# Cross-attention and mixture-of-experts layer: the residual travels with the scattered token rows and is added on VectorE instead of by an accumulating scatter

## The reference

```python
x = x + _L0_xattn_ref(_layernorm(x), ctx_1024, Wq1, Wk1, Wv1, Wk2, Wv2, Wo, bo)
x = x + _L0_ffn_ref(_layernorm(x), shared_w1, shared_w2, expert_w1, expert_w2, router_w, ln_gamma, ln_beta)
# _L0_ffn_ref:
h = (x - mu) / jnp.sqrt(var + LN_EPS) * ln_gamma + ln_beta
shared_out = jax.nn.silu(h @ sw1.T) @ sw2.T            # sw, ew: weights rounded to -1, 0, 1 times a row scale
probs = jax.nn.softmax(h @ router_w.T, axis=-1)
gate = one_hot(argmax(probs)) * max(probs)
h1 = jax.nn.silu(jnp.einsum('btd,efd->ebtf', h, ew1))
eo = jnp.einsum('ebtf,edf->ebtd', h1, ew2)
return shared_out + jnp.einsum('ebtd,bte->btd', eo, gate)
```

## Time and profile before

| what | us |
|---|---|
| median of 3 runs (lowest to highest) | 825.51 (825.13 to 829.35) |
| the profiled execution's own time | 822.83 |
| its span | 821.0 |
| PE busy | 674.1 (82%) |
| DVE busy | 640.7 (78%) |
| ACT busy | 586.1 (71%) |
| POOL busy | 578.7 (70%) |

### The profile page before, as it was taken

One profiled execution on the slowest core, in us unless ns is written; L12 is line 12 of the kernel. 1 busy time (PEld: TensorE's weight loads), 2 busy tenths in 40 slices (PEclk: granted clock), 3 DMA queues, 4 the chain that ended last, 5 costly groups with the idle time before them and its releaser, 6 DMA issues.

```text
span 821.0 us, 22257 instructions
## 1 busy us (share of the span) xinstructions
PE 674.1 (82%) x7738; PEld 471.7 (57%) x7738; DVE 640.7 (78%) x1411; ACT 586.1 (71%) x1324; POOL 578.7 (70%) x684
## 2 busy tenths in 40 slices
PE   3689779899989998999889898989997555777883
PEld 2355546666666666666656565766664343655652
DVE  3878768889888988788888888888977647676873
ACT  3668667888787878788787878787876622665662
POOL 1356557787878778697888787878877755365664
PEclk9989999999999999999999999999998877899997
DMA  7289867898998998979998889999795913699991
GB/s 256 39 170 161 174 125 151 167 172 184 171 173 169 167 180 170 187 156 181 175 175 166 162 172 170 175 179 177 138 165 136 165 45 119 129 143 142 149 132 15
DMA packets 367523, 126.87 MB, mean 155 GB/s; under 512 B 331114, under 2 KB 362740, under 8 KB 367412
## 3 DMA queue, kind: packets, MB, share of 16 engines
q1 hardware_dynamic: 359604, 116.11, 74.2%
q0 software_dynamic: 7232, 8.79, 7.2%
q10 hardware_dynamic: 576, 0.54, 0.2%
HBM read 30.71 MB, written 14.71 MB: 55 GB/s over the span
## 4 chain that ended last, share of the span: by engine, by line
PE 31%; DVE 20%; issue 14%; DMA 11%; SPq 9%; ACT 8%; POOL 6%; DVEq 0%; ACTq 0%; POOLq 0%
PE FB L358 10%; DMA pt<-p_split 8%; PE TBK L1463 4%; DVE neg_max L1208 4%; PE S L1391 4%; SPq L514 4%; POOL p_split L582 3%; ACT p_split L784 2%; DVE FB L946 2%; SPq L507 2%; DVE above L951 2%; ACT k_st L747 2%; DVE v_st L976 2%; DVE hn L1058 2%; SPq L508 2%
## 5 line engine op out<-in xcount | busy, mean ns | idle before, releaser
L582 POOL TENSOR_TENSOR p_split<-probs,p_split 128x512 f16<-128x512 f32 x256 | 300.6, 1183 | 62.8 <-ACT p_split L784 60.2
L822 ACT ACTIVATE probs<-S,neg_max 128x512 f32<-128x512 f32 x256 | 175.3, 685 | 16.1 <-DVE neg_max L1208 14.8
L784 ACT ACTIVATE p_split<-probs 128x512 f16<-128x512 f32 x256 | 161.1, 629 | 16.0 <-DMA pt<-p_split 14.5
L1208 DVE TENSOR_REDUCE neg_max<-S 128x1 f32<-128x512 f32 x256 | 171.1, 679 | 0.3
L358 PE MATMUL FB<-xt_hi,w_split 128*128 128x256 f16 x768 | 141.6, 276 | 3.2 <-DVE xt_lo L973 2.9
L1407 PE MATMUL O<-v_st,pt 128*128 128x64 f16 x1024 | 114.8, 195 | 23.0 <-DMA pt<-p_split 22.9
L1407 PEld LDWEIGHTS O<-v_st,pt 128*128 128x128 f16 x1024 | 93.3, 99 | 56.4 <-DMA pt<-p_split 32.8
L1408 PE MATMUL O<-v_st,pt 128*128 128x64 f16 x1024 | 114.1, 194 | 0.0
L1409 PE MATMUL O<-v_st,pt 128*128 128x64 f16 x1024 | 114.1, 194 | 0.0
L1391 PE MATMUL S<-k_st,q_st 64*128 64x512 f16 x768 | 107.1, 385 | 1.1 <-ACT probs L822 1.1
L358 PE MATMUL FB<-xt_lo,w_split 128*128 128x256 f16 x384 | 105.8, 276 | 0.0
(11 more groups left out here) (223 smaller groups left out, 1752.4 us busy)
## 6 DMA issues: line engine op xcount, KB each, us to landing
w_raw<-in_L_ffn_expert_w SPq DMA_DIRECT2D x16, 512.0 KB, 4.4
w_split<-rows SPq DMA_DIRECT2D x39, 132.0 KB, 2.5
c_in<-in_ctx SPq DMA_DIRECT2D x16, 256.0 KB
x_in<-in_x SPq DMA_DIRECT2D x16, 256.0 KB
xb<-in_x SPq DMA_DIRECT2D x16, 256.0 KB, 3.3
pt<-p_split SPq DMA_TRANSPOSE x256, 3.3
out<-rest SPq DMA_DIRECT2D x15, 256.0 KB, 2.7
k_st<-in_L_xattn_Wk SPq DMA_DIRECT2D x2, 512.0 KB, 7.1
```

The source lines that it names most:

```text
L582: g.tensor_tensor(p_split[n % HL_RING][:, 1, :], probs[n % PROBS_RING][:, :], p_split[n % HL_RING][:, 0, :], ALU.subtract).then_inc(p_lo_r ...
L784: a_(p_split[g % HL_RING][:, 0, :], probs[g % PROBS_RING][:, :], ACT.Copy).then_inc(p_hi_ready, 1)
L822: a_(probs[n % PROBS_RING][:, :], S[n % 4][:, :], ACT.Exp, bias=neg_max[:, n % 4:n % 4 + 1], accum_out=sums[:, n % UNITS:n % UNITS + 1]).t ...
L1208: v.tensor_reduce(neg_max[:, n % 4:n % 4 + 1], S[n % 4][:, :], AX.X, ALU.max, negate=True)\
```

## The change

The rows in device memory become twice as wide: HALF = 264 floats as before, and behind them another 264 that begin with the token's residual part. `rest` is gone: DVE and POOL write the residual part into `row`, and it is scattered with the rest of the row. The stores of the residual part to `out` are gone (L496, L699), so nothing is in `out` before the expert stage; DVE adds the residual part to each tile's result (`add_residual`) and POOL scatters it without adding. `scatter_rows` now needs the residual part, so the table moves the scatters of the last batch but one (EARLY_SCATTER 44 to 46). The last batch is scattered in two halves: the first half at once, the residual half when it is ready. The ring of row buffers has the same memory and so half the places (RING 16 to 8). Tiles 0 to 7 are loaded by halves, the first by SP, the second by POOL behind the last scatter; the others by SP as one load of 264 KB. The zero rows are twice as wide too. In the expert stage ACT scales three of the four chunks and DVE one.

```diff
-RING = 16
+RING = 8
-EARLY_COUNT, EARLY_RANKS, EARLY_PLACE, EARLY_SCATTER = 40, 41, (42, 43), 44
+EARLY_COUNT, EARLY_RANKS, EARLY_PLACE, EARLY_SCATTER = 40, 41, (42, 43), 46
-    rows = nc.dram_tensor("rows", [E * ROOM, WIDTH], F32, kind="Internal").ap()
+    rows = nc.dram_tensor("rows", [E * ROOM, 2 * HALF], F32, kind="Internal").ap()
...
-                t = due(n, STORE_R)
-                if t is not None and t < B - 1:
-                    sp.wait_ge(r_ready, t + 1)
-                    sp.dma_start(out_v[t], rest[t % 2][:, :, :]).then_inc(r_stored, 16)
...
             def load_rows(a):
                 at = sp.value_load(tile_row[0:1, bass.ds(a, 1)], min_val=0, max_val=E * ROOM - P)
-                sp.dma_start(g_rows[a % RING], rows[bass.ds(at, P), :]).then_inc(row_in[a % RING], 16)
+                cols = HALF if a < RING else 2 * HALF
+                sp.dma_start(g_rows[a % RING][:, 0:cols], rows[bass.ds(at, P), 0:cols]).then_inc(row_in[a % RING], 16)
...
-                sp.dma_start(rows[bass.ds(at, P), :], zeros).then_inc(padded, 16)
+                sp.dma_start(rows[bass.ds(at, P), :].rearrange("p (k c) -> p k c", k=2), pad_rows).then_inc(padded, 16)
...
                     if a + LEAD >= RING:
+                        if a + LEAD == RING:
+                            sp.wait_ge(r_scattered, 16 * TB)
                         sp.wait_ge(e_out, a + LEAD - RING + 1)
...
+                    pool.wait_ge(r_ready, t + 1)
                 scatter(row[t % 2][:, i, :], rows, dest_at[:, t * TB + i:t * TB + i + 1], E * ROOM - 1)\
                     .then_inc(scattered[t % 2], 16)
...
             pool.wait_ge(r_ready, B)
-            g.dma_start(out=out_v[B - 1], in_=rest[(B - 1) % 2][:, :, :]).then_inc(last_r_stored, 16)
-            pool.wait_ge(r_stored, 16 * (B - 1))
-            pool.wait_ge(last_r_stored, 16)
+            pool.wait_ge(halves_ready, 2)
+            for i in range(TB):
+                scatter(row[(B - 1) % 2][:, i, HALF:2 * HALF], half_rows, half_at[:, 1, i:i + 1], 2 * E * ROOM - 1)\
+                    .then_inc(r_scattered, 16)
...
+            pool.wait_ge(r_scattered, 16 * TB)
+            for a in range(RING):
+                at = pool.value_load(tile_row[0:1, a:a + 1], min_val=0, max_val=E * ROOM - P)
+                g.dma_start(out=g_rows[a][:, HALF:2 * HALF], in_=rows[bass.ds(at, P), HALF:2 * HALF]).then_inc(rest_in[a], 16)
             for a in range(SLOTS):
                 pool.wait_ge(e_id, a + 1)
                 pool.wait_ge(e_out, a + 1)
-                g.indirect_dma_start(out=out, out_offset=bass.IndirectOffsetOnAxis(ap=slot_idx[:, a:a + 1], axis=0),
-                                     in_=e_res[a % OUTS], in_offset=None, bounds_check=B * T - 1, oob_is_err=False,
-                                     compute_op=ALU.add).then_inc(stored[a % OUTS], 16)
+                scatter(e_res[a % OUTS], out, slot_idx[:, a:a + 1], B * T - 1).then_inc(stored[a % OUTS], 16)
...
-                                       ALU.mult, ALU.mult).then_inc(e_out, 1)
+                                       ALU.mult, ALU.mult).then_inc(e_y, 1)
+            def add_residual(a):
+                if a < RING:
+                    dve.wait_ge(rest_in[a], 16)
+                dve.wait_ge(row_in[a % RING], 16 * (a // RING + 1))
+                dve.wait_ge(e_y, a + 1)
+                v.tensor_tensor(e_res[a % OUTS], e_res[a % OUTS], g_rows[a % RING][:, HALF:HALF + D], ALU.add).then_inc(e_out, 1)
...
             def down(a, s, e):
                 pe.wait_ge(e_g_lo, a + 1)
                 if not (is_static(a) and a < 2):
-                    pe.wait_ge(e_out, a - 1)
+                    pe.wait_ge(e_y, a - 1)
```

More of the change, by code:

```diff
@@ L165, in xattn_ffn @@
         hn = sb("hn", [P, TB, D], F32)
-        row = [sb(f"row{i}", [P, TB, WIDTH], F32) for i in range(2)]
-        rest = [sb(f"rest{i}", [P, TB, D], F32) for i in range(2)]
+        row = [sb(f"row{i}", [P, TB, 2 * HALF], F32) for i in range(2)]
+        half_at = sb("half_at", [P, 2, TB], U32)
         ht = sb("ht", [P, TB, 2 * DC, P], F16)
@@ L268, in xattn_ffn @@
         scattered = [sem(f"scattered{i}") for i in range(2)]
-        r_stored = sem("r_stored")
-        last_r_stored = sem("last_r_stored")
+        halves_ready = sem("halves_ready")
+        h_scattered = sem("h_scattered")
+        r_scattered = sem("r_scattered")
+        rest_in = [sem(f"rest_in{i}") for i in range(RING)]
         zeroed = sem("zeroed")
@@ L362, in xattn_ffn @@
         c_v = ctx_in.rearrange("b (t p) d -> b p t d", p=P)
-        out_v = out.rearrange("(b t p) d -> b p t d", p=P, t=TB)
+        half_rows = rows.rearrange("n (k c) -> (n k) c", k=2)
         ew1_v = ew1.rearrange("e (c p) d -> e p c d", p=P)
@@ L547, in _ @@
             for a in row:
-                g.memset(a[:, :, D:WIDTH], 0.0).then_inc(const_ready, 1)
+                for half in range(2):
+                    g.memset(a[:, :, half * HALF + D:(half + 1) * HALF], 0.0).then_inc(const_ready, 1)
             g.iota(expert_down[:, :], [[-1, E]], base=E, channel_multiplier=0,
@@ L622, in scatter_rows, with scatter_last_heads @@
                     pool.wait_ge(h_lo_ready, t + 1)
+                    pool.wait_ge(r_ready, t + 1)
                 scatter(row[t % 2][:, i, :], rows, dest_at[:, t * TB + i:t * TB + i + 1], E * ROOM - 1)\
                     .then_inc(scattered[t % 2], 16)
+            def scatter_last_heads():
+                pool.wait_ge(placed, B * 2)
+                g.tensor_scalar(half_at[:, 0, :], dest[:, :], 2.0, None, ALU.mult).then_inc(halves_ready, 1)
+                g.tensor_scalar(half_at[:, 1, :], dest[:, :], 2.0, 1.0, ALU.mult, ALU.add).then_inc(halves_ready, 1)
+                pool.wait_ge(halves_ready, 1)
+                pool.wait_ge(prob_ready, B)
+                pool.wait_ge(named, B)
+                pool.wait_ge(h_lo_ready, B)
+                for i in range(TB):
+                    scatter(row[(B - 1) % 2][:, i, 0:HALF], half_rows, half_at[:, 0, i:i + 1], 2 * E * ROOM - 1)\
+                        .then_inc(h_scattered, 16)
             def gate_scale(t, j):
@@ L639, in _ @@
                     pool.wait_ge(shared_ready, t + 1)
-                    r = rest[t % 2][:, :, :]
+                    r = row[t % 2][:, :, HALF:HALF + D]
                     g.tensor_tensor(r, r, x2[t % 2][:, :, :], ALU.add).then_inc(r_ready, 1)
@@ L863, in scale_high @@
                     act.wait_ge(e_g, a - 1)
-                for c in range(2):
-                    last = a_(e_up[s][:, (2 + c) * P:(3 + c) * P], S[2 + s][:, c * P:(c + 1) * P], ACT.Copy,
+                for c in range(3):
+                    last = a_(e_up[s][:, (1 + c) * P:(2 + c) * P], S[2 + s][:, c * P:(c + 1) * P], ACT.Copy,
                               scale=tile_scale[:, a, c:c + 1])
@@ L1173, in list_absent @@
                 also(v.tensor_copy(absent_id, absent))
-                for c in range(2):
-                    last = v.tensor_tensor(scale_terms[:, c, :, :], owner, spread(up_scale[:, 0:E, 2 + c], EA, 1), ALU.mult)
+                for c in range(3):
+                    last = v.tensor_tensor(scale_terms[:, c, :, :], owner, spread(up_scale[:, 0:E, 1 + c], EA, 1), ALU.mult)
                 then(last)
-                for c in range(2):
+                for c in range(3):
                     last = v.tensor_reduce(tile_scale[:, :, c], scale_terms[:, c, :, :], AX.X, ALU.add)
@@ L1316, in step @@
                     name_slot(k - 2)
+                if tile_in_range(k - 3):
+                    add_residual(k - 3)
             tiles(dve, step)
```

47 lines of the change are left out of this document (27 added, 20 removed).

## The result

The changed kernel is slower: 853.25 us in the median of four runs (851.23 to 854.15) against 827.36 for the kernel before in the same session, a ratio of 1.031 (95% interval 1.0271 to 1.035), some 26 us. Forecast were 833.2 and at most 841. The direction was right, the size wrong by a factor of more than three (+7.7 against +25.9).

What follows compares the result with a forecast made beforehand. SP's issue at 2.73 us a tile was taken to pace the expert stage, with PE busy 557 of 640 us in the batch stage. Terms 0 + 2.6 + 2.2 + 0.9 + 4.0 - 2.0 = +7.7 gave 833.2 us; 8-in-10 range 827 to 841.

Steps and rivals of the forecast that it cites:

- The loop of the ring: Expert stage, tiles 6 to 36: period 2.87 us against 2.734, +4.0 us, bounds -3.3 and +11.4.
- The circle: Expert stage from tile 6: transpose, up-projection, scalings, residual add, SP's load of a+5, transpose of a+3; length x + 3.80.
- x: Time from a tile's transpose start to its `gate_up` start on DVE; read as 5.54 and 4.07, taken as 4.8 us.
- 3.80: Rest of the three-tile loop, `gate_up` start to the next transpose: 2.02 - 0.13 + 0.49 + 0.05 + 0.91 + 0.46 us.
- The relief: Expert stage DMA: plain scatters cut about a sixth of a tile's traffic, so transposes land sooner; x taken as 4.8.
- DVE and ACT: Expert stage: ACT's 128 more columns and DVE's add and later register load fit in idle time; 0 us.
- rival C: Expert stage: x stays at 5.54, loop +11.4, +15.1 in all, 840.6 us; chance 0.14 shared with another rival.
- The scatters past the count: End of batch stage: POOL's two scatters now stand ahead of the last batch's count; +2.6 us, bounds +1.5 and +3.4.
- The wider pads: Passage to the expert stage: another 1.08 MB of pads delays SP's first register load; +2.2 us, between 0.5 and 3.2.
- Start of the ring: Expert stage start: tile 8's load, ahead of tile 6's transpose, waits for tile 0's result; +0.9 us, bounds 0 and +3.
- The batch stage: Some 650 us: stores gone, scatters twice as wide, DMA share stays, PE covers; 0 us, bounds -3 and +3.
- The end: Last tiles: POOL's queue of accumulates goes, so the last scatter starts sooner and is shorter; -2.0 us, bounds -3 and 0.

Runs made afterwards that it cites:

- the narrow loads: Changed kernel with tiles 8 to 38 loading only the first 132 KB of their rows, their residual left out of the result: ratio 1.025 to the kernel before.
- the register load moved: Changed kernel with DVE's register load of the next tile's expert ahead of the residual add instead of behind it: ratio 1.023 to the kernel before.
- the kernel without the add: Changed kernel without the residual add, the scaling signalling the tile; loads stay wide and the ring at 8: ratio 1.019 to the kernel before.
- 12 buffers: Changed kernel with 12 row buffers instead of 8, the four more in memory of their own: ratio 1.012 to the kernel before.
- the one with the transpose first: Kernel before with SP issuing the transpose of tile a ahead of the load of tile a+2: ratio 1.006 to the kernel before.
- The mended order: Changed kernel with the last-but-one batch's scatters behind the last count and zero rows written in two halves: ratio 1.034 to the kernel before.
- the kernel with the transpose and the register load first: Changed kernel with SP's transpose ahead of the load and DVE's register load ahead of the residual add: ratio 1.014 to the kernel before.

## Why the prediction was wrong, step by step

**The loop of the ring is the step that failed.** The circle was named rightly, and its formula holds: (x + 3.80) / 3 with the measured x of 6.07 is 3.29, and 3.35 was measured; for the narrow loads 3.27 against 3.28. That the 3.80 is met is partly luck: in the changed kernel's means its parts are 1.94, 0.53, 0.06, 0.81 and 0.46, with DVE's two 0.09 longer than priced and the way from the register load to the DMA 0.10 shorter. The term was mis-sized, +4.0 where it measured +18.4, and outside its own upper bound of +11.4. Three errors went the same way, and two readings under them were wrong.

*The slack and SP's own pace.* I read a slack of 0.23 us between the end of tile 22's result (770.94) and the start of tile 30's load (771.17). But the wait for a buffer stands ahead of the register load, and that starts at 770.38: the slack was -0.56. Over tiles 11 to 38 it would have been -0.49 in the mean, and negative for 24 of 28, so the ring of 8 was too short before anything was added. And I put SP's own work at 2.58 a tile and the rest of the 2.73 down to the transposes' landing. By the means it is 2.73 with no wait in it: the transpose's issue took 1.27 in the mean and not 1.21, the way to the load's DMA 0.04 more, and 0.05 stands behind the transpose. A relief on the landing could therefore shorten nothing of the period before.

*The relief.* I took x = 4.8, between 5.54 and 4.07, because a sixth of the DMA traffic goes. The traffic went, and more than I said. But the kernel before with plain scatters shows what that is worth: x falls by 0.08. The quick transpose of tile 1 was no measure of it. The middle was a guess: the sum of engine time gave no figure for x. The mean of before (5.31) would have been the better base: (5.31 + 3.80) / 3 = 3.04, +9.1.

*x grows with the change.* It went up by 0.76: 0.27 to PE's start, of which the narrow loads give back 0.26; 0.13 in the up-projection, beside a granted clock of 0.90 instead of 0.97; 0.36 because DVE isn't ready when PE is. I had set "DVE and ACT" to 0, with the register load behind the add named but not priced: my terms give 2.02 + 0.45 = 2.47 for DVE's step, and it is 2.82. The experiments say more of the bounds than of the parts, though. With the register load moved, DVE's 0.3 came back as waiting for the transpose, so the three parts cannot be added up as independent causes.

*A circle with no slack passes on every late landing.* In all six kernels with a ring of 8 and the load first the measured period lies over the formula's, by 0.01 to 0.16 (the old kernel with a ring of 8: (5.43 + 3.44) / 3 = 2.96 against 3.06). The formula takes SP to be waiting at every tile. In the old kernel with a ring of 8 it is not: its register load starts 0.37 us after the result's end in the mean and not 0.05, which is 0.11 of a period and covers the gap. With 16 buffers the x of single tiles ran from 4.37 to 6.28 (tiles 7 to 36) and SP never paused for it. I wrote that late landings are passed on under rival C and did not put it into the sum.

Split by experiments, in this order, the 0.61 a tile are 0.33 for the ring of 8 alone, 0.25 for the add inside the circle, and 0.03 for what else the kernel without the add has over the ring alone (wide loads, plain scatters, three chunks on ACT). The three are one chain: without the ring's circle (12 buffers) all but 0.07 is gone, and with it what the add costs.

**The scatters past the count: right.** +2.6 forecast from the order and four rows, +2.6 measured, 6.0 against 3.4 before. Of the other old kernels two have 3.4 and the one with the transpose first 4.2, for which no run shows the reason. The mended order gave back 1.8.

**The wider pads: too small.** +2.2 forecast, +3.6 measured, over my upper bound of 3.2. I counted the added bytes at 336 GB/s, which is 3.2, and then took off cover that isn't there. The DMA engines were at 0.97 to 1.01 and 338 to 346 GB/s from 694 to 700 us. Of the 3.6, 1.6 lie ahead of the last pad's issue (6.4 us from the copy of the counts instead of 4.8) and 2.0 in its landing (4.39 instead of 2.43). The estimate of 2.5 us by the Trainium skill's 436 GB/s (DMA: Bandwidth & Descriptors, Anatomy of one DMA) is short too; the page gives that fit for DMAs that GpSimd issues, and these are SP's and ACT's. The trace decides.

**Start of the ring: right,** +0.9 against +0.8; POOL's residual halves came in time.

**The batch stage: right, with a warning.** Its end is 4.6 us later in the profile, but the old kernel's batch stage, unchanged, ends at 680.9, 683.3, 684.4 and 686.3 in four profiles, and that of ten profiles of changed kernels at 682.1 to 687.2. A difference of 4.6 can't be told from spread between executions. The medians differ by 25.9, which fits 31.0 less 4.6.

**The end: wrong sign.** POOL's queue went as forecast: the last scatter starts 1.9 us after its result's scaling instead of 3.0. But three tiles still drain behind the transpose of tile 36, and from there to the last scaling it takes 18.0 us instead of 15.9. That DVE's longer step and PE's lower clock make it so is argued, not shown apart.

Of the rivals C was nearest (840.6), and still 13 too low. The marks I had set came out: SP's loads wait for the residual add (26 of 31), the software share is under 20%, POOL doesn't queue; tiles 6 to 36 span 100 us and not the 86 that I set. No mark was set for x, the number on which the term hung.

## What to carry to other kernels

A ring of buffers is a circle of waits: its length is the time from the load that takes a buffer to the result that frees it, over the tiles that may be between. Read its slack at the instruction that carries the wait (here the register load, some 0.8 us or more ahead of the DMA), and over many tiles: where it is negative, as here by 0.5 us, the smaller ring costs at once, before anything is widened. Each instruction put between the result and the freeing signal then costs a share of itself per tile. Before pricing a relief, add up the steps of the engine that sets the pace; if they fill the period without a wait, no faster transfer shortens it. When sizing such a term, take the mean over many tiles and add what the change does to every part of the circle; a relief elsewhere counts only if a row shows that the part shortens with it. Before you drop a ring's depth to make room, ask what frees a buffer, and whether a second, smaller ring for the new data would leave the first alone; that version was not run.

## What the runs showed of the hardware

An accumulating scatter of 128 rows held the 16 DMA engines 2.7 times as long as a plain one (software share 44.5% against 16.6% over 60 us), and POOL 1.56 against 0.98 us, but PE had a transposed tile hardly later: 3.96 us from the transpose's start against 3.82. DMA share alone said little of latency: at 0.69 this time was 4.23 us in the changed kernel, at 0.89 it was 3.96 before.

SP's issue of the same 128x512 transpose took 1.21 us in the median of the kernel before, 1.99 at most, and up to 2.97 in the kernel with the transpose and the register load first. The mean over tiles 6 to 35 ran from 1.27 to 1.46 in the fourteen profiles. Where SP had no pause, these tenths were tenths of the period.

A register load on an engine's queue waited behind a compute instruction that itself waited for a semaphore. In the changed kernel (DVE's register load, ns min/median/max, then two of DVE's instructions) the load is hardly longer than before (313 in the median), but it starts only at 758.31, once the add has been let go, and DVE idles 0.72 us. At least 0.40 us of such idle time stands in every tile:

```profile
L343 DVEq TENSOR_LOAD <-v_st x39: 300/343/680, 707.8 to 833.4; - x39
```

```profile
758.28 0.42 DVE L1334 TENSOR_TENSOR w_raw<-w_raw,w_split 128x256 f32<-128x256 f32 x1
759.43 0.29 DVE L1307 TENSOR_TENSOR x<-S,up_scale 128x128 f32<-128x128 f32 x1 [0.72 <-issue]
```
